# Two attentions and two feed-forward blocks on one core: a ring of five single score banks, one batch of values a group, causal masks by GpSimd

## What is computed

```python
x = x + attn_a(_layernorm(x))   # 16 heads of 16, softmax over a band of +-32 and 4 global tokens
x = x + ffn(_layernorm(x))      # silu(x wg) * (x wu) @ wd, hidden 768
x = x + attn_b(_layernorm(x))
x = x + ffn(_layernorm(x))
# attn_b, per head:
num = jnp.exp(jnp.einsum('bhqd,bhkd->bhqk', q_rot, k_rot) * scale)
den = jnp.sum(jnp.exp(jnp.einsum('bhqd,bhkd->bhqk', q, k) * scale), axis=-1, keepdims=True)
attn = num / den
attn = jnp.where(causal[None, None], attn, 0.0)
y = jnp.einsum('bhqk,bhkd->bhqd', attn, v)
```

## Time and profile before

| | |
|---|---|
| median of three runs | 2621.99 us (2620.69 to 2629.52) |
| profiled execution, its own time | 2629.34 us |
| its span, first to last instruction | 2627.4 us |
| PE busy | 2165.7 us |
| ACT busy | 1446.6 us |
| DVE busy | 1403.2 us |
| POOL busy | 600.8 us |
| mean granted TensorE clock | 0.890 |

### The profile page before, as it was taken

One profiled execution on the slowest core, in us unless ns is written; L12 is line 12 of the kernel. 1 busy time (PEld: TensorE's weight loads), 2 busy tenths in 40 slices (PEclk: granted clock), 3 DMA queues, 4 the chain that ended last, 5 costly groups with the idle time before them and its releaser, 6 DMA issues.

```text
span 2627.4 us, 73355 instructions
## 1 busy us (share of the span) xinstructions
PE 2165.7 (82%) x27269; PEld 1471.7 (56%) x27269; DVE 1403.2 (53%) x2972; ACT 1446.6 (55%) x3580; POOL 600.8 (23%) x619
## 2 busy tenths in 40 slices
PE   2577889889897988989898888979888898988785
PEld 2355456566565655656566565656556565655454
DVE  3355456464655646465564646556564555645433
ACT  1224656556465655746565564656566465656571
POOL 0013131222223113221311322231222223122311
PEclk7679889989898998989899998989999898988886
DMA  4223334142422414243241424324142422423221
...
DMA packets 130030, 203.13 MB, mean 77 GB/s; under 512 B 27057, under 2 KB 60849, under 8 KB 129601
## 3 DMA queue, kind: packets, MB, share of 16 engines
...
...
## 4 chain that ended last, share of the span: by engine, by line
issue 52%; PE 17%; POOL 13%; DVE 6%; ACT 5%; DMA 4%; SPq 2%; POOLq 0%; ACTq 0%; DVEq 0%
POOL h L1558 7%; PE gu_bank L1010 3%; ACT s_bank L1137 2%; DMA xn<-o_scr_B 2%; POOL tmp L1563 2%; PE d_bank L1026 2%; PE o_bank L942 2%; POOL x L1553 2%; PE gu_bank L985 1%; PE gu_bank L1038 1%; POOL root L1545 1%; PE gu_bank L975 1%; SPq L519 1%; PE s_bank L920 1%; PE s_bank L886 1%
## 5 line engine op out<-in xcount | busy, mean ns | idle before, releaser
L1137 ACT ACTIVATE s_bank<-s_bank 128x512 f32<-128x512 f32 x1024 | 603.8, 590 | 206.9 <-PE s_bank L899 206.3
L1127 ACT ACTIVATE probs_B<-s_bank 128x512 f32<-128x512 f32 x640 | 344.3, 600 | 214.1 <-PE s_bank L927 213.7
L1558 POOL TENSOR_TENSOR h<-tmp,h 128x512 fp32r<-128x512 f32 x192 | 245.1, 1276 | 845.7 <-DVE h L1422 845.7
L1404 DVE SCALAR_TENSOR_TENSOR tmp<-tmp,gu_bank 128x512 f32<-128x512 f32 x192 | 131.6, 686 | 402.8 <-ACT tmp L1166 402.8
L899 PE MATMUL s_bank<-pack_b 48*128 48x512 f16 x1024 | 209.5, 415 | 75.7 <-ACT s_bank L1137 54.4
L1010 PE MATMUL gu_bank<-xT,w_g 128*128 128x256 f32 x1536 | 236.6, 293 | 6.0 <-DVE tmp L1404 3.6
L1010 PE MATMUL gu_bank<-xT,w_u 128*128 128x256 f32 x1536 | 236.7, 293 | 0.4 <-DVE tmp L1410 0.4
L1026 PE MATMUL d_bank<-w_d,h 128*128 128x256 f32 x1536 | 230.0, 292 | 6.9 <-POOL h L1558 6.9
L1010 PEld LDWEIGHTS gu_bank<-xT,w_g 128*128 128x128 f32 x1536 | 198.8, 190 | 34.8 <-issue 21.2
L1010 PEld LDWEIGHTS gu_bank<-xT,w_u 128*128 128x128 f32 x1536 | 198.2, 190 | 25.7 <-issue 17.6
L1026 PEld LDWEIGHTS d_bank<-w_d,h 128*128 128x128 f32 x1536 | 194.5, 188 | 31.9 <-issue 19.8
(11 more groups left out here) (145 smaller groups left out, 3475.9 us busy)
## 6 DMA issues: line engine op xcount, KB each, us to landing
pack_b<-src_b SPq DMA_DIRECT2D x768, 64.0 KB, 2.6
pack_a<-src_a SPq DMA_DIRECT2D x384, 64.0 KB, 2.3
...
```

The costliest lines, as they stand in the source:

```text
L1127: act.activation(probs["B"][:, n % RING, :], score_bank(s, "N", n // 2, n % 2)[:, :], ACT.Exp, scale=SM_SCALE)\
L1137: act.activation(bank[:, :], bank[:, :], ACT.Exp, scale=SM_SCALE, accum_out=den[:, 0, j, 2 * tile + e, t:t + 1]).then_inc(den_exp, 1)
L1404: dve.scalar_tensor_tensor(t, t, 1.0, gu_bank[0][:, :], ALU.add, ALU.mult).then_inc(gu_taken, 1)
L1558: pool.tensor_tensor(h[1][:, i % 2, :], tmp[:, i % 2, :], h[0][:, i % 2, :].bitcast(F32), ALU.subtract)\
```

## The change

1. `o_bank` becomes a fifth score bank. The ring goes round bank by bank: a step takes one bank (DT, BV) or two (the others), and waits for whoever had just those banks last (`users_before`). For a row of steps that take two each, that is the second bank of the step three before and the first bank of the step two before.
2. The values of a group of attention b are one batch (BV0 to BV3), in a bank of the ring, behind all five pairs of the group and their masks. `probs["B"]` has ten tiles, one group's; the first exponential of a group waits for the values of the group before (`b_used`).
3. PE's mask matmuls go. POOL zeroes the probabilities above the diagonal instead, after the exponential: a new step **CM p** (`mask_pair`), one `affine_select` on 128x2x128 f32 for each piece of a pair, 32 a turn. The values wait for `b_masked`.
4. The table is another: every number in it, so the order on all engines.

The constant tiles `causal` and their two loads, and the clearing of `o_bank` ahead of the loop, go too.

```diff
-BATCH_B = [(0, 1, 2, 3), (4, 5, 6, 7), (8, 9)]
-RING = 8
+RING = {"A": 8, "B": NU_B}
 AT = {
...
-    "BV": (33.64, 36.75, 40.06, 58.91, 59.11, 61.93, 75.66, 81.98, 82.94, 111.04, 121.46, 0),
+    "CM": (1.98, 2.37, 3.64, 1.4),
+    "BV": (42.98, 67.27, 92.71, 0),
...
+BANKS = 5
+TAKEN = {"A1": 2, "TM": 2, "A2": 2, "AV": 2, "D": 2, "DT": 1, "N": 2, "BV": 1}
...
+    return (earlier(s.k) + sum(TAKEN[k] for k, _ in s.items[:s.items.index((kind, n))])) % BANKS
...
+def users_before(s, kind, n):
+    found = []
+    for e in range(1 if kind == "TM" else TAKEN[kind]):
+        bank = e - BANKS
+        for o, k, m, first in steps_before(s, kind, n):
+            if first <= bank and k == "TM" and bank > first:
+                bank -= BANKS
+            elif first <= bank:
+                found.append((o, k, m, bank - first))
+                break
+    return found
...
             def pair_free(s, kind, n, turn):
-                found = item_before(s, kind, n)
...
-                    pe.wait_ge(den_exp, (b * UNITS["D"] + 2 * (n + 1)).at(turn))
...
+                for o, kind, n, e in users_before(s, kind, n):
...
+                        pe.wait_ge(den_exp, (b * UNITS["D"] + (2 * n + e + 1)).at(turn))
...
+                    elif kind == "BV":
+                        pe.wait_ge(o_taken, (o.take("B", n)[0] + 1).at(turn))
...
-                for i in range(pieces):
-                    for half in range(2):
-                        for e in range(2):
-                            c0 = UNITS_B[n + e][i][2]
-                            last = pe.matmul(bank[e][HB * half:HB * half + HB, c0:c0 + P], eye_of(e), rows_of(causal, e, half),
-                                             start=False, stop=True, tile_position=(HB * e, HB * half), skip_group_check=True)
...
+            def b_values(s, block, j, turn):
+                bank = score_bank(s, "BV", j)
+                pair_free(s, "BV", j, turn)
+                if j == 0:
+                    pe.wait_ge(gu_taken, (s.gu("VB") + 2).at(turn))
+                pe.wait_ge(b_masked, (s.seq[block] * PAIRS_N + (j + 1) * (NU_B // 2)).at(turn))
...
+                if i == 0 and (j or seq.some):
+                    act.wait_ge(b_used, (seq * GROUPS + j).at(turn))
...
-                dve.tensor_copy(o_raw[at][:, :], o_bank[:, :]).then_inc(o_taken, 1)
+                dve.tensor_copy(o_raw[at][:, :], score_bank(s, "BV", j)[:, :]).then_inc(o_taken, 1)
...
+            def mask_pair(s, p, turn):
+                pool.wait_ge(b_exp, (s.seq["B"] * UNITS["N"] + 2 * (p + 1)).at(turn))
+                pool.sem_inc(mask_open, 1)
+                n = 2 * p % NU_B
+                for _, _, c0 in UNITS_B[n]:
+                    a = probs["B"][:, n:n + 2, c0:c0 + P]
+                    ins = pool.affine_select(a, a, [[0, 2], [1, P]], ALU.is_ge, 0.0, base=0, channel_multiplier=-1)
+                ins.then_inc(b_masked, 1)
```

133 lines of the change are left out of this document (60 added, 73 removed), and 40 rows, old and new, of the table AT.

## The result

The changed kernel takes 2671.22 us (median of four, 2657.53 to 2673.26) against 2625.76 us of the kernel before measured beside it (four runs, 2620.69 to 2635.72): a ratio of 1.0158, 95% interval 1.0122 to 1.0194. It is slower by 1.6%, where 2560 us had been forecast. A second measurement on another chip, further down, gives 1.0087 (1.0054 to 1.0119): slower again, but by 0.9%, and the two intervals do not meet. So the size of the loss is known only as 0.9 to 1.6%. The profiled execution took 2669.25 us, with a span of 2667.2 us and a mean granted clock of 0.874, against 2629.34, 2627.4 and 0.890.

A forecast was written before the change was run, and what follows sets the result against it. PE was taken to bound the third and fifth stretch, ACT the fourth, DVE beside PE the second. Gains of 4.0 us a turn over 16 turns, less 2.5 us at the end, gave 2560 us, range 2530 to 2590.

The forecast's parts named there:

- The masks leave PE: PE's mask matmuls go: 4.4 us a turn, 1.1 in the second stretch, 2.2 third, 0.4 fourth, 0.7 fifth.
- the third and fifth stretch: Parts of a turn, 53 and 15 us long, with PE taken as the bound; gains of 2.5 and 1.0 us.
- The first stretch: First 36 us of a turn, attention b's rotation and the projections, paced by a chain of engines; gain 0.
- The joins: Twelve value batches in ten places become four: six joins at 0.13 us each, 0.8 us a turn.
- the ring: Five banks: 1.0 us gained a turn at the fourth stretch's end, 0.5 lost to D11 in the second.
- the fourth stretch: 18 us of a turn, paced by ACT with the last denominators; 1.0 us gain taken, bounds 0 and 2.3.
- D11 waits 1.0 us for the copy: Second stretch: D11 needs BV0's bank, so waits 1.0 us for DVE's copy BT0; charged 0.5 us a turn.
- The values wait for no select: Values stand far enough behind their group's last select in the loop; nothing charged for lateness.
- The end, 2.5 us: At the program's end no other sequence covers the last batch and selects: some 2.5 us lost once.
- DVE held for 0.7 us in the second stretch: One in six of eight selects there holds DVE for 0.5 us: 0.7 us lost a turn, ends 0 and 5.8.
- The rivals: DVE held half the time: 2.9 us, 2596 us, chance 0.19; DVE held every time: 10.2 us, 2712 us, chance 0.09.
- The extra waits of `pair_free`: One more wait a pair, 66 more small instructions on PE's queue in a turn, priced at nothing.

## Why the prediction was wrong, by its steps

Two steps failed most: the masks' work was counted as time on PE, and the new order was priced at nothing.

- **The masks leave PE, 4.4 us a turn**, counted almost in full: this step failed, with the reading "PE is the bound" of the third and fifth stretch under it. Measured with nothing else changed, a turn is no shorter without the masks, in the order of before (150.4 us with, 151.2 without) or in the new (153.6, 153.9). From BV0 to BV2 the gain is -0.2 us, where 2.2 had been counted for the third stretch. The matmuls did leave: PE's busy time fell by 2.3 us a turn, with 3 us more of the turn at 1.2 GHz. But PE, busy 94% of that stretch, was not its limit: its gate matmuls waited 24.6 us for DVE in place of 12.8. That DVE's part of the feed-forward was next in line by less than the masks' length fits these waits; no run with a shorter DVE part tried it.
- **The first stretch: 0; the order unpriced.** This is the other failed step. The places of D11, BT0, BV0 and N16 were priced and no others, though every number in the table had moved. Exchanged alone, the table costs 1.2 to 1.9% in the new structure with selects, and 1.6% with PE's masks (1.0033, 0.9876). The largest new wait, VA's 3.8 us a turn, was to be seen in the order of DVE's steps, T22 and T23 behind the splits, but it is not the whole price: a kernel with 4.5 us of it lies at 1.0038, and taking most of it away brought 0.6 to 1.3%. With PE's masks the loss lies from the head's values to BV0 (1.8 us a turn) and from BV0 to BV1 (1.7 us). Which moved step makes it there stays open.
- **The joins, 0.8 us, and the ring, 1.0 less 0.5**: too small together, and for other reasons than given. The new structure in the order of before, with PE's masks, is 3.1 us a turn shorter (150.4 against 153.5). The 1.0 us that the ring was to bring at the end of the fourth stretch did not come: N16 and N17 follow DT as foreseen, but DT waits for ACT instead, and N17 is 0.2 us nearer to N15. This is the low bound of the prediction, "if ACT alone sets the end". What came instead: the stop of 1.6 us in attention a's values went, which is in no term of the sum, and D pairs wait 1.3 us less. Taken apart, the joins and the ring are +2% and -3.2%: the joined batch is a loss without the fifth bank.
- **D11 waits 1.0 us for the copy**, charged at 0.5: it waits 1.25, more than the 1 us that was named as a sign of being wrong.
- **A select takes 0.5 us**: 0.407. **POOL 53 us a turn**: 50.9. **The values wait for no select**: right in the loop.
- **The end, 2.5 us**: the two waits for a select there are 5.8 us, as no other sequence runs. The three shorter turns behind the loop are 20.7 us longer in all, half of what the profiled execution lost. The kernels with four banks and one part of the change (masks by POOL, new order) take 386.9 and 387.3 us for these three turns, where the kernel before has 379.1 and the changed one 399.8; why is open.
- **DVE held for 0.7 us in the second stretch**: right in place and nearly in size, 0.5. The rivals had 2.9 and 10.2 us of it; 0.5 us was enough, since it came on top of a wait of 1.5 us, and in the turns with 2.0 us PE's granted clock was lower behind it every time. The Trainium skill, "GPSIMD Engine Reference", section "Key points", has the contention that these rows show. By it alone I had worked out 4 us, and most operations met no select: the median of the layer norm's operation is 403 ns with selects and 405 without.
- **The extra waits of `pair_free`: nothing.** No run contradicts it; it was not tried by itself.

In ratios, the change is -1.2% for ring and joins, +0.9% for the masks' move and +1.9% for the order (0.9876, 0.9965, 1.0158; +1.2% with 1.0087), where the sum had -0.7% (1.1 us a turn), -1.7% (2.9 us a turn, less the 2.5 at the end) and 0.
